# Fused gated cross-attention layer: order of the fold units, and which engine bounds the weights

## What is computed

```python
q, k, v = LN(x) @ Wq, ctx @ Wk, ctx @ Wv            # Wq 512x1024, Wk and Wv 384x1024
x = x + tanh(g_xattn) * (softmax(q k^T / 8) v @ Wo + bo)
x = x + tanh(g_ffn) * (LN(x) @ W[idx] + b[idx])     # idx = argmax(log_softmax(logits) + gumbel(u))
```

## Time and profile before

| | us |
|---|---|
| median of 3 runs (lowest, highest) | 1044.67 (1043.48, 1044.71) |
| the profiled execution | 1044.16 |
| its span | 1042.4 |
| TensorE busy in the span | 1027.5 |
| VectorE, ScalarE, GpSimd busy | 847.8, 749.1, 443.0 |
| first score matmul (L1405) starts in the span at | 87.89 |

### The profile page before, as it was taken

One profiled execution on the slowest core, in us unless ns is written; L12 is line 12 of the kernel. 1 busy time (PEld: TensorE's weight loads), 2 busy tenths in 40 slices (PEclk: granted clock), 3 DMA queues, 4 the chain that ended last, 5 costly groups with the idle time before them and its releaser, 6 DMA issues.

```text
span 1042.4 us, 21853 instructions
## 1 busy us (share of the span) xinstructions
PE 1027.5 (99%) x6074; PEld 587.0 (56%) x6074; DVE 847.8 (81%) x1800; ACT 749.1 (72%) x2720; POOL 443.0 (42%) x637
## 2 busy tenths in 40 slices
PE   9998999999999999999999999999999999999998
PEld 7634455555555555555555555555555555555555
DVE  4677988888888888888888887888888887888876
ACT  3778877777677677776777677766776677767761
POOL 1686344444443344444433344444433344444422
PEclk9999999999999999999999999999999999999999
DMA  8414566665566665665566666655566656655656
GB/s 323 101 21 111 107 127 125 143 126 125 111 134 137 139 135 125 141 123 114 117 137 136 136 134 129 142 119 111 128 137 136 136 126 138 136 116 111 133 110 142
DMA packets 383073, 135.02 MB, mean 130 GB/s; under 512 B 361930, under 2 KB 362750, under 8 KB 382974
## 3 DMA queue, kind: packets, MB, share of 16 engines
q1 hardware_dynamic: 382974, 134.09, 59.8%
HBM read 27.48 MB, written 16.78 MB: 42 GB/s over the span
## 4 chain that ended last, share of the span: by engine, by line
PE 89%; DVE 4%; ACT 3%; DMA 2%; SPq 1%; issue 1%; POOL 0%; DVEq 0%; ACTq 0%
PE banks L1405 82%; PE banks L1638 3%; ACT work L902 1%; PE banks L1515 1%; DMA fold_area<-in_L_xattn_Wo 1%; PE banks L1451 1%; PE banks L1523 1%; PE banks L1504 1%; DVE work L449 1%; ACT vw_area L850 0%; DMA work<-work 0%; DVE vw_area L1110 0%; DVE fold_area L1121 0%; DVE red L1030 0%; DVE work L1209 0%
## 5 line engine op out<-in xcount | busy, mean ns | idle before, releaser
L902 ACT ACTIVATE work<-banks,red,cst 128x77 f32<-128x77 f32 x1024 | 410.3, 430 | 83.3 <-DVE red L1200 83.2
L1405 PE MATMUL banks<-fold_area,work 128*128 128x456 f16 (+1 forms) x2304 | 405.4, 335 | 2.8 <-DMA work<-work 2.0
L1405 PE MATMUL banks<-vw_area,work 128*128 128x512 f16 x1674 | 371.4, 379 | 0.9 <-DMA work<-work 0.9
L1405 PEld LDWEIGHTS banks<-fold_area,work 128*128 128x128 f16 x2304 | 225.2, 98 | 171.4 <-DMA work<-work 2.9
L1405 PEld LDWEIGHTS banks<-vw_area,work 128*128 128x128 f16 x1674 | 163.6, 98 | 186.0 <-DMA work<-work 1.8
L449 DVE SCALAR_TENSOR_TENSOR work<-work 128x256 f16<-128x256 f32 (+3 forms) x443 | 240.8, 578 | 1.3 <-ACT work L798 0.6
L902 ACT ACTIVATION_READ_ACCUMULATOR work<-banks,red,cst 128x1 f32 x1024 | 224.5, 219 | 0.0
L1198 DVE TENSOR_REDUCE stats<-banks 128x6 f32<-128x462 f32 (+1 forms) x192 | 112.1, 584 | 102.3 <-PE banks L1405 102.2
L1405 PE MATMUL banks<-work 128*128 128x256 f16 x1302 | 162.4, 272 | 0.7 <-DVE work L1285 0.5
L1405 PEld LDWEIGHTS banks<-work 128*128 128x128 f16 x1302 | 126.8, 98 | 31.8 <-DVE work L1285 0.7
L733 POOL TENSOR_TENSOR stats<-stats,cst 128x1 f32<-128x1 f32 x64 | 12.6, 196 | 281.5 <-DVE stats L1234 281.5
(11 more groups left out here) (150 smaller groups left out, 818.0 us busy)
## 6 DMA issues: line engine op xcount, KB each, us to landing
work<-in_x SPq DMA_DIRECT2D x64, 256.0 KB, 2.8
out<-work SPq DMA_DIRECT2D x63, 256.0 KB, 2.2
work<-work SPq DMA_TRANSPOSE x253, 3.1
fold_area<-in_L_xattn_Wo SPq DMA_DIRECT2D x4, 512.0 KB, 9.1
work<-in_L_ffn_W SPq DMA_DIRECT2D x2, 1024.0 KB, 8.4
fold_area<-in_L_xattn_Wq SPq DMA_DIRECT2D x2, 1024.0 KB, 14.5
fold_area<-in_L_xattn_Wv SPq DMA_DIRECT2D x3, 512.0 KB, 6.5
fold_area<-in_L_xattn_Wk SPq DMA_DIRECT2D x2, 768.0 KB, 12.3
```

Source lines behind the costliest of these rows:

```text
L902: nc.scalar.activation(probs_of(place, place + 1), s_heads(m, k)[:, h - h0, :], ACT.Exp, bias=nmx[:, h:h + 1], scale=exp_scale, accum_out= ...
L1405: mm = nc.tensor.matmul(ps, lhs(l), rhs(r), start=first and n == 0, stop=last and n == 2, skip_group_check=onto)
```

## The change

The bookkeeping lines of `FROM`, `PARTS` and the index of `power_of_two` follow from it and are in the diff.

- New head of `VISITS`: all four PROJECT come first, then REMAINDER 0, SPREAD 0, TURN 0, VALUE 0, REMAINDER 1, KEY 0 and 1, VALUE 1, REMAINDER 2, TURN 1, VALUE 2, REMAINDER 3, VALUE 3, SPREAD 1. From place 18 (KEY 2) on the list is as before; SPREAD 1 stands where a PASS stood.
- SPREAD 0 spreads KK and WQ; SPREAD 1, ten places later, spreads WF.
- The spread of VV follows PROJECT 1 instead of PROJECT 0.
- Half of Wq is now bounded on VectorE (a maximum, at PROJECT 2), the ffn matrix on ScalarE (two `Abs` sums, at PROJECT 3).
- `copy_k(1)` stands ahead of the scaling of the values on ScalarE, `key_part(0)` right after `largest(VV)` on VectorE.
- `x_scale(0, 0)` on GpSimd moves from REMAINDER 1 to REMAINDER 2, `x_moments(0, 0)` from PROJECT 3 to KEY 1, `x_low(0, 0)` from KEY 1 to VALUE 3.

```diff
-        FROM = [0, 6, 11, 16, 21]
-        PARTS = [5, 4, 4, 4, 1]
+        FROM = [0, 6, 11, 16, 20]
+        PARTS = [5, 4, 4, 3, 2]
...
-        VISITS = [(PROJECT, 0), (PROJECT, 1), (PROJECT, 2), (REMAINDER, 0), (VALUE, 0), (PROJECT, 3), (REMAINDER, 1), (VALUE, 1),
-                  (SPREAD, 0), (TURN, 0), (REMAINDER, 2), (VALUE, 2), (REMAINDER, 3), (KEY, 0), (KEY, 1), (VALUE, 3), (TURN, 1),
-                  (PASS, 0), (KEY, 2), (KEY, 3), (VALUE, 4), (PASS, 1), (KEY, 4), (KEY, 5), (VALUE, 5), (TURN, 2), (KEY, 6), (KEY, 7), (VALUE, 6),
+        VISITS = [(PROJECT, 0), (PROJECT, 1), (PROJECT, 2), (PROJECT, 3), (REMAINDER, 0), (SPREAD, 0), (TURN, 0), (VALUE, 0),
+                  (REMAINDER, 1), (KEY, 0), (KEY, 1), (VALUE, 1), (REMAINDER, 2), (TURN, 1), (VALUE, 2), (REMAINDER, 3), (VALUE, 3),
+                  (SPREAD, 1), (KEY, 2), (KEY, 3), (VALUE, 4), (PASS, 1), (KEY, 4), (KEY, 5), (VALUE, 5), (TURN, 2), (KEY, 6), (KEY, 7), (VALUE, 6),
...
-                if (kind, n) == (REMAINDER, 1):
+                if (kind, n) == (REMAINDER, 2):
                     x_scale(0, 0)
...
-            def query_bounds(half):
+            def query_bounds():
                 act.wait_ge(floor_set, 1)
-                act.wait_ge(wq_loaded[half], 16)
+                act.wait_ge(wq_loaded[0], 16)
                 act.wait_ge(v_done, HP)
-                for k in (2 * half, 2 * half + 1):
-                    nc.scalar.activation(wv_raw[:, k, :] if k < CT else fold_area[:, A_WORDS + CT * ID:A_WORDS + CT * ID + ID], wq_raw[:, k, :],
-                                         ACT.Abs, accum_out=part_of(WQ, k)).then_inc(parts_ready[WQ], 1)
+                for k in range(KT // 2):
+                    nc.scalar.activation(wv_raw[:, k, :], wq_raw[:, k, :], ACT.Abs, accum_out=part_of(WQ, 1 + k)).then_inc(parts_ready[WQ], 1)
+            def ffn_bounds():
+                act.wait_ge(wf_loaded, 16)
+                for n, junk in enumerate((wv_raw[:, CT - 1, :], fold_area[:, A_WORDS + CT * ID:A_WORDS + CT * ID + ID])):
+                    rows = wf_raw[:, n * KT // 2:(n + 1) * KT // 2, :].rearrange("p k n -> p (k n)")
+                    nc.scalar.activation(junk, rows, ACT.Abs, accum_out=part_of(WF, n)).then_inc(parts_ready[WF], 1)
             copy_k(0)
+            copy_k(1)
             act.wait_ge(scale_v_ready, 1)
...
                 if t == 0:
-                    act.wait_ge(parts_ready[WF], 1)
+                    act.wait_ge(parts_ready[WF], PARTS[WF])
...
-                if kind == PROJECT and n > 0:
+                if kind == PROJECT and n > 1:
                     copy_k(n)
+                if (kind, n) == (PROJECT, 2):
+                    query_bounds()
+                if (kind, n) == (PROJECT, 3):
+                    ffn_bounds()
...
-                if (kind, n) == (PROJECT, 2):
-                    query_bounds(0)
-                if (kind, n) == (VALUE, 0):
-                    query_bounds(1)
...
             largest(VV)
+            key_part(0)
             power_of_two(VV, 3)
...
-            dve.wait_ge(wf_loaded, 16)
-            part(WF, 0, wf_raw)
-            largest(WF)
-            key_part(0)
             key_part(1)
...
+                if (kind, n) == (PROJECT, 2):
+                    dve.wait_ge(wq_loaded[1], 16)
+                    part(WQ, 0, wq_raw[:, KT // 2:KT, :])
+                    largest(WQ)
                 if (kind, n) == (PROJECT, 3):
                     largest(KK)
-                    largest(WQ)
-                if kind == SPREAD:
+                if (kind, n) == (SPREAD, 1):
+                    power_of_two(WF, pair_of(SPREAD, 1))
+                if (kind, n) == (SPREAD, 0):
...
-                    power_of_two(WF, first, P)
-                if (kind, n) == (PROJECT, 3):
+                if (kind, n) == (KEY, 1):
+                    largest(WF)
                     x_moments(0, 0)
                     dve.wait_ge(x_stats, 1)
                     x_variance()
-                if (kind, n) == (KEY, 1):
+                if (kind, n) == (VALUE, 3):
                     x_low(0, 0)
...
-                    for m in (KK, WQ, WF):
+                    for m in (WF,) if n else (KK, WQ):
                         pe.wait_ge(pow_step[m], 1)
...
-                if (kind, n) == (PROJECT, 0):
+                if (kind, n) == (PROJECT, 1):
                     spread(VV, 3)
...
-                if kind == SPREAD:
-                    spread(WF, pair_of(SPREAD), P)
+                if (kind, n) == (SPREAD, 1):
+                    spread(WF, pair_of(SPREAD, 1))
+                if (kind, n) == (SPREAD, 0):
                     spread(KK, pair_of(SPREAD))
                     spread(WQ, pair_of(SPREAD) + 1)
```

## The result

The changed kernel takes 1046.82 us (median of 12 runs, 1046.30 to 1048.54), the kernel before, timed beside it, 1044.52: ratio 1.0023, 95% interval 1.0015 to 1.0031, that is 2.4 us slower (1.6 to 3.2). 1047.5 was forecast, +2.9.

The account below looks back on a forecast made before the run. TensorE bounds the kernel (busy 1027.5 of 1042.4 us), so prologue delays pass to the end: VALUE 4 at 53.1 instead of 50.23, +2.9 on the 1044.67 median, gives 1047.6, stated as 1047.5; range over the cases 1044.8 to 1049.0.

Parts of the forecast that it names:

- One number decides, VALUE 4's start: End of the prologue: everything later follows the VALUE chain, so VALUE 4 moving from 50.23 to 53.1 costs +2.9 us.
- The wait at SPREAD 0: Prologue: TensorE arrives at 34.2, waits 1.2 us for VectorE until 35.4, and the 0.79 us gain is gone.
- The new wait: ScalarE at `x_normalized(0, 0)`: stands still 2.5 us, from about 47.0 to 49.55, for GpSimd's scale queued behind `side_split(2)`.
- the walk: Prologue: each engine followed through the new list with the profile's durations, putting VALUE 4 at 53.1 us.
- The size: Whole kernel: +2.9 us, from VALUE 4's later start, carried to the end.
- the spread of VV: TensorE's head: 0.32 us between PROJECT 1 and PROJECT 2, ending at 26.1, 2.3 us later than before.
- four ScalarE steps: Behind the wait for the scale: x normalized 0.82, REMAINDER 3's copies 0.92, `x_high` 0.64, VALUE 3's copy 1.04 us.
- ScalarE's bounds of the ffn matrix: Prologue: two bounds done by 35.1, REMAINDER 0's copies by 36.1, wanted only at about 37.8; cost nothing.
- GpSimd catches up: Behind VALUE 4: REMAINDER 3's split starts 4.3 us later, 1.4 more than the rest; 10 us of idle time absorb it.
- the fourth case: Rival, clock falls in a pause: some 5 us of prologue at 1.2 GHz, +4.2 on top, 1050.5 us; chance 0.03.

Follow-up runs that it names:

- The later bias block: Changed kernel with VectorE's three bias instructions moved from ahead of the third key part to behind VALUE 0's low part: 1046.08 us, ratio 1.0015.
- Moving one line back: Changed kernel with only `x_scale(0, 0)` on GpSimd back at REMAINDER 1: 1044.71 us, ratio to the kernel before 1.0002.
- the variant with longer pauses: Kernel before with only `x_scale(0, 0)` moved from REMAINDER 1 to REMAINDER 2: 1050.24 us, ratio 1.0057; second trace 1049.66 us.

## Why the prediction was right, and where its size was off

- **One number decides, VALUE 4's start.** Right: 2.45 us there, at VALUE 5 and at the first scores, and 2.5 in the span.
- **The wait at SPREAD 0.** Forecast 1.2 us, measured 1.04, released by `largest`. The later bias block took it out, and 0.88 us of it reached the first scores.
- **The new wait.** Forecast 2.5 us ahead of L791 until 49.55; measured 2.48 until 49.59. The length is right; that the moment agrees to 0.04 us is luck: the head was 0.86 us later than in the trace the walk started from, and the walk up to there 0.8 us too long. Moving one line back gave 2.3 us aligned and made the kernel level with before.
- **The size.** +2.9 was forecast, +2.4 measured as a ratio of medians; but of the trace's 2.45 us, 0.86 is the head, so the order of the work itself costs 73.21 less 71.5 (the mean of the three), 1.7 us.
- **The mis-sized step** is the sum of terms in a row. VALUE 4 was put 53.1 - 16.27 = 36.8 us behind the first copy and came 52.68 - 17.13 = 35.55 behind it. Of these 1.3 us, 0.6 lie ahead of SPREAD 0, put 19.1 us behind the first copy and met at 18.53; in it are 0.2 for the spread of VV, charged 0.32 where it held the projections up by about 0.1. From SPREAD 0 to the end of REMAINDER 2 the walk charged 8.5 us and the timeline has 8.2 (35.66 to 43.84): REMAINDER 1 with KEY 0 and 1 took 3.01 instead of 3.17, SPREAD 0 with TURN 0 1.21 instead of 1.34. From the scale's end to VALUE 4 the walk charged 3.42 + 0.15 us for four ScalarE steps; the timeline has 49.55 to 52.68, 3.1, for each starts about 0.1 us ahead of the recorded end of the last. The error of the walk and the head's scatter had opposite signs, so the forecast looks closer than the walk was.
- **ScalarE's bounds of the ffn matrix.** Costed at nothing, right: REMAINDER 0's copies ended at 36.5, REMAINDER 1 began at 37.89 without a wait.
- **GpSimd catches up.** Right: no shift grows behind VALUE 4.
- **The clock.** The fourth case did not come; its mechanism did, in the variant with longer pauses. The Trainium skill (TensorE: Matmul & The Clock Gate, "HAM oscillation") says that an idle gap puts TensorE back to half rate when it is long enough, and those traces agree, with 0.50 behind a pause of 2.3 us, once with 1.5 more. There it cost TensorE 1.6 us in the one trace, where the fourth case had +4.2. Behind 1.39 and 0.64 us the changed kernel stayed at 1.00.

## What to carry to other kernels

When a small step is moved to a later visit on one engine, look at who asks for it in program order, and count everything queued behind that instruction: here 1.2 us of tiny GpSimd operations behind a 3.4 us split held four ScalarE steps and a pair of banks. Such a wait is better cured by producing early than by asking late, where the later place has no idle time either (some 0.5 us here, by the traces). When medians differ by 2 us, align the traces at a point that the change can't have touched, take each kernel's trace more than once, and see how far that point scatters.

## What the runs showed of the hardware

A pause of TensorE of 2.3 us, in one trace with 1.1 us of work and 1.5 us of pause behind it, in the other with nothing but work, was followed by a granted clock of 0.50 for some 3 us in the first and some 7 us in the second. In the first the clock cost TensorE some 0.86 us on KEY 2 and 3 (2.15 against 1.29) and 0.78 on VALUE 4. Pauses of 1.04, 1.39 and 0.64 us left it at 1.00.

The first copy of the values scatters by 1.3 us (16.27 to 17.53) from trace to trace of nearly the same program, more than most single edits here moved. It comes from TensorE's own first matmuls, 12 of which take 0.96 to 1.75 us with no idle time around them.
